# The first phase's TensorE queue: the projection of q issued ahead of two groups of transposes

## The reference

```python
h = _layernorm(x, axis=-1)
q_in = silu(causal_dwconv(h @ Wq, wq_conv))      # 4 taps
k_in = silu(causal_dwconv(h @ Wk, wk_conv))
v_in = silu(causal_dwconv(h @ Wv, wv_conv))
beta = sigmoid(h @ Wb)
q = l2norm(q); k = l2norm(k)
kb = k * beta[..., None]                         # the scaled keys
local_short = causal_dwconv(v_in, fir_short)     # 5 taps
```

## Time and profile before

| | before |
|---|---|
| median of 3 runs | 1263.83 us |
| lowest, highest | 1260.26, 1267.31 us |
| the profiled execution, own time | 1260.86 us |
| its span | 1259.1 us |
| granted TensorE clock over the span | 0.949 |
| PE, DVE, ACT, POOL busy | 1084.3, 984.7, 755.2, 645.1 us |

### The profile page before, as it was taken

The page is one execution under the profiler, slowest core; times in us unless marked ns, Lnnn a source line. Parts: engine busy times, 40 slices in busy tenths (PEclk is TensorE's granted clock), DMA queues, the critical chain, the costliest instruction groups (busy, mean ns, idle before and its releaser), DMA issues. The chain is left out here.

```text
span 1259.1 us, 28322 instructions
## 1 busy us (share of the span) xinstructions
PE 1084.3 (86%) x8715; PEld 793.7 (63%) x8799; DVE 984.7 (78%) x2955; ACT 755.2 (60%) x1456; POOL 645.1 (51%) x2360
## 2 busy tenths in 40 slices
PE   5798988596788989999999999999999977875755
PEld 4677767494456666777777677677777744542224
DVE  4899989696776887988888888898888778624975
ACT  5787878533344456666666766766666553435766
POOL 4777776415356564665656555565565644001006
PEclk9988988798899999999999999999999998897979
DMA  5666766546224254334335435434532532115006
GB/s 163 212 206 199 229 197 184 188 123 169 80 68 122 82 138 140 92 108 148 95 114 149 119 117 149 126 107 124 149 93 81 161 97 61 43 40 187 1 7 227
DMA packets 159830, 160.33 MB, mean 127 GB/s; under 512 B 65320, under 2 KB 126656, under 8 KB 159680
## 3 DMA queue, kind: packets, MB, share of 16 engines
q1 hardware_dynamic: 155552, 157.47, 41.6%
q10 hardware_dynamic: 4128, 1.05, 0.4%
HBM read 96.34 MB, written 61.87 MB: 126 GB/s over the span
## 5 line engine op out<-in xcount | busy, mean ns | idle before, releaser
L2154 DVE CUSTOM_DVE_ANT_0 x_psA<-x_psA,x_mask_q 128x256 f32<-128x256 f32 x496 | 200.6, 446 | 60.0 <-PE x_psA L1438 59.1
L1706 ACT ACTIVATE x_PT<-x_psB 128x512 f32<-128x512 f32 x240 | 143.6, 598 | 143.1 <-PE x_psB L1465 141.8
L314 DVE SCALAR_TENSOR_TENSOR a_conv<-a_ps_proj,taps,a_conv 128x253 f32<-128x253 f32 (+2 forms) x288 | 115.0, 470 | 16.7 <-ACT a_conv L381 16.7
L537 PE MATMUL a_ps_proj<-a_hT,wqkv 128*128 128x256 f32 x384 | 108.4, 432 | 9.5 <-DVE a_conv L314 6.6
L1438 PE MATMUL x_psA<-x_Ks,x_Qs 96*128 96x256 bf16 x496 | 97.6, 278 | 15.5 <-DVE x_maxima L2154 13.3
L1465 PE MATMUL x_psB<-x_Qs,x_Ks 98*128 98x256 bf16 x480 | 93.0, 274 | 10.5 <-issue 5.9
L537 PEld LDWEIGHTS a_ps_proj<-a_hT,wqkv 128*128 128x128 f32 x384 | 80.0, 219 | 29.7 <-issue 14.6
L2154 DVE DVE_READ_ACCUMULATOR2_ANT x_maxima<- 128x1 f32 x512 | 72.0, 141 | 0.0
L1479 PE MATMUL x_psO<-x_PT,x_V 128*32 128x256 f32 x1024 | 71.1, 397 | 0.7 <-ACT x_PT L1706 0.7
L2377 POOL TENSOR_TENSOR f_y<-f_y,f_x 128x512 f32<-128x512 f32 x16 | 22.9, 1454 | 87.8 <-DVE f_y L2365 80.2
L1465 PEld LDWEIGHTS x_psB<-x_Qs,x_Ks 98*128 98x128 bf16 x480 | 47.6, 99 | 32.0 <-issue 1.4
(11 more groups left out here) (385 smaller groups left out, 3256.7 us busy)
## 6 DMA issues: line engine op xcount, KB each, us to landing
scratch_keypack<-a_keypack SPq DMA_DIRECT2D x16, 768.0 KB, 3.8
c_keypack<-scratch_keypack SPq DMA_DIRECT2D x16, 768.0 KB, 4.6
x_Ks<-scratch_k_parts SPq DMA_DIRECT2D x192, 64.0 KB, 2.4
matrix<-scratch_taps_copies SPq DMA_DIRECT2D x32, 256.0 KB, 4.0
scratch_k_parts<-x_parts_k SPq DMA_DIRECT2D x32, 192.0 KB, 2.3
scratch_q_parts<-x_parts_q SPq DMA_DIRECT2D x32, 192.0 KB, 2.5
x_Qs<-scratch_q_parts SPq DMA_DIRECT2D x32, 192.0 KB, 2.9
a_x_in<-in_x SPq DMA_DIRECT2D x16, 256.0 KB, 3.7
```

The costliest lines, as they stand in the source:

```text
L314: nc.vector.scalar_tensor_tensor(acc, ps_proj[PROJ_BANK[p]][:, c, 0:L - j], taps[:, p, c, TAPS - 1 - j:TAPS - j], acc, ALU.mult, ALU.add). ...
L537: last = nc.tensor.matmul(ps_proj[PROJ_BANK[p]][:, o], wqkv[:, p, c, o * P:(o + 1) * P], hT[par][:, c], start=c == 0, stop=c == FC - 1)
L1706: nc.scalar.activation(PT[:, k % (2 * GROUP)], bank_B(b, k)[0], ACT.Exp, scale=XD ** -0.5).then_inc(pexp_ready, 1)
L2154: last = nc.vector.tensor_tensor_reduce(bank_A(b, k)[0][:, s], bank_A(b, k)[0][:, s], mask_q[:, t], 1.0, LOWEST, ALU.add, ALU.max, maxima[ ...
```

## The change

The entry of `proj_q` leaves the top of `A_ORDER`, where it stood as `(3, "proj_q")` between `kpk` and `tap_q`, and comes back as `(2, "proj_q")` between `short_t` and `stok`. Stage 2 instead of 3 and a place late in the list instead of early in the next turn mean the same batch in the same round: it is issued once per batch as before, only ahead of what used to stand between, on PE the transposes `ksT` and `tok1`. Nothing is added or removed. The rest of the difference only breaks the list's lines anew.

```diff
 A_ORDER = [
-           (5, "kpk"), (3, "proj_q"), (3, "tap_q"), (3, "conv_k"), (4, "tail"),
+           (5, "kpk"), (3, "tap_q"), (3, "conv_k"), (4, "tail"),
...
-           (4, "short_t"), (4, "stok"), (1, "xn"), (2, "gbias"), (4, "ks"), (4, "ksT"), (3, "tok1"), (3, "sq1"),
+           (4, "short_t"), (2, "proj_q"), (4, "stok"), (1, "xn"), (2, "gbias"), (4, "ks"), (4, "ksT"), (3, "tok1"), (3, "sq1"),
```

More of the change, by code:

```diff
@@ L70, in rsqrt @@
         nc.gpsimd.tensor_tensor(y, y, t, ALU.mult).then_inc(step, 1)
-A_ORDER = [(0, "ld_x"), (1, "copy"), (4, "silu_v"), (1, "rstd"), (5, "kpk"), (3, "proj_q"), (3, "tap_q"), (3, "conv_k"), (4, "tail"),
+A_ORDER = [(0, "ld_x"), (1, "copy"), (4, "silu_v"), (1, "rstd"), (5, "kpk"), (3, "tap_q"), (3, "conv_k"), (4, "tail"),
            (4, "norms"), (4, "norm"), (2, "turn_h"), (2, "hTc"), (4, "ktok"), (5, "st_p"), (4, "st_k"), (3, "taps0"),
[L77 to L80, removed]
+           (3, "conv_q"), (5, "diag"), (4, "stap"), (5, "dk"), (3, "tanh"), (3, "silu_q"), (2, "proj_k"), (4, "short1"),
+           (3, "silu_k"), (3, "proj_v"), (3, "tap_v"), (4, "tok2"), (4, "vtok"), (2, "tap_k"), (2, "gate"), (0, "stat"),
+           (4, "short2"), (3, "st_hT"), (3, "gsc"), (4, "st_v"), (4, "win"), (3, "taps1"), (3, "tok0"), (3, "sq0"),
+           (4, "short_t"), (2, "proj_q"), (4, "stok"), (1, "xn"), (2, "gbias"), (4, "ks"), (4, "ksT"), (3, "tok1"), (3, "sq1"),
            (4, "st_s"), (3, "conv_v")]
```

## The result

| | before | changed |
|---|---|---|
| median of the runs | 1265.45 us (4 runs) | 1306.39 us (4 runs) |
| lowest, highest | 1260.26, 1267.31 | 1296.52, 1310.29 |
| profiled execution, span | 1259.1 us | 1304.1 us |
| first matmul of `phase_b` | 248.2 us | 288.1 us |

The change makes the kernel slower: ratio 1.0319, 95% interval 1.028 to 1.0358, 41 us by the medians. I had forecast slower, at 1283 us, and the range ended at 1297. The direction was right; the forecast size, 21 us, was half of what came.

What follows compares the result with a forecast made beforehand. No engine is full; in the first phase they wait for one another in a ring. To 1260.9 us it added 10 (longer ring) and 11 (PE's lower clock), giving 1282; forecast 1283, range 1271 to 1297.

Steps and rivals of the forecast that it cites:

- the ring: First phase, `conv_q` to next `conv_q` through `conv_v`, `proj_q`, `ksT`, `tok1`, `sq1`, `tap_q`: 14.20 us at full clock, +10 us.
- the list of steps: The steps from one `conv_q` start to the next at full clock, from 6.42 us up to `conv_v` on, summing to 14.20 us.
- slow turns: First-phase turns with PE at its lower clock in `ksT`, `tok1`, `proj_q`: 1.68 us more each, 11 of 14 before.
- `conv_q` to the start of `conv_v`, DVE's own work without a wait: 6.42 us: First step of a first-phase turn, on DVE, taken from the trace before the change: 6.42 of 14.20 us.
- POOL sets the pace: Rival: POOL's 14.86 us from `ks` to `ks`, with a stall under DVE's `short1`, sets each turn; 1283 us, chance 0.06.
- the clock, +11: PE's lower clock in the first phase, up to 1.68 us a turn, taken in a bit under half of 14 turns.
- Every turn slow: Rival: PE's lower clock costs 1.68 us in each of 14 first-phase turns; +33.5 us, 1294; chance 0.17 (nearly all slow).
- Faster: Rival: DVE's 13.8 us wait for `tap_q` goes because the product comes first; at best 1247 us, chance 0.04.
- No turn slow: Rival: PE keeps its full clock in all or most first-phase turns; +10 to +14 us, 1271 to 1275; chance 0.17 (few slow).

Runs made afterwards that it cites:

- the square: Changed kernel with `gsc` unmoved or moved, PE idle or kept busy by unread matmuls: `phase_b` starts at 288.1, 267.8 (idle), 268.6, 258.4 us (busy).

## Why the prediction was wrong

**Right: the ring, its members and its length.** Of the list of steps only the first failed. `conv_v` to `conv_q` was 7.78 us in the sum (14.20 - 6.42) and 7.80 in the trace; the whole ring 14.20 against 14.27 in the kernel with `gsc` moved and PE kept busy; its cost over the 15 gaps +10 against +11.0 (20.64 to 232.77 us there, 212.1 against 211.2). This cost is net of the 10.6 us that the slow turns of the kernel before had taken, as in the prediction's own sum, which set full-clock turns against the 201.1 us as they were. That `tap_q` is queued behind `sq1` is shown by the ACT rows, and that the ring runs through `tok1` by the kernel with `tok1` first, which gives all of the loss back, and by 12.83 against 14.27 us a turn at full clock.

**Wrong: "`conv_q` to the start of `conv_v`, DVE's own work without a wait: 6.42 us".** It was 7.27 us in eleven turns. I took DVE's part of a turn as fixed, although the change shifts POOL's work against it: `gsc` now meets `ks` and ends only with it, 0.86 us a turn, 9.4 us by count, 10.2 by the square. I had contention only as the rival "POOL sets the pace", a DVE instruction holding a POOL one, and priced it as hidden. It came the other way round, on the engine that has no slack. `ks` began at 174.06 and ended at 175.44, `gsc` ended at 175.46. The page "SBUF — State Buffer" of the Trainium skill, section "Who interferes with whom", says that the pair of SBUF ports that VectorE and GpSimd share is an exclusive lock, that `tensor_scalar` can take it in its faster modes, and that issue order decides who blocks. The trace agrees: `ks` was first, and `gsc` ended 0.02 us behind it.

**Mis-sized: the clock, +11.** The parts above 7.80 us from `conv_v` to `conv_q` sum to 19.4 us over twelve turns. With the contention the clock cost 19.5 us. Without it, it cost 9.4 by the profiled executions, near the 11, and 2 by the medians. What failed is the share of slow turns: I took a bit under half of 14, and twelve of fifteen were slow; with `gsc` moved, five. Why the contention makes more turns slow is not shown. It lengthens the turn (15.08 against 14.26 us at full clock) and PE's wait (2.78 against 1.85 us), but by the turns named above neither of the two alone decides. "Every turn slow", to which I gave 0.17, was the better guess here, and even its +33.5 lacked the contention.

Without the contention the forecast would have stood: the kernel with `gsc` moved has `phase_b` 19.6 us later than before and a median 16 us above, and I had said 21. That is partly luck, since nothing in the rows of before fixed how many turns would be slow. The later phases took 5 us more in the profiled execution; no cause was shown.

**The other rivals.** That the clock's part was paid before as well is true of about half of it (10.6 of 19.5 us). Faster: refuted by the order on ACT, as argued; `sq1` came too late in each turn. No turn slow: refuted. POOL's pace: refuted for the changed kernel, where POOL waits 47.8 us, though POOL does set the turns of the kernel before once the clock is full.

## What to carry to other kernels

Issuing a result earlier is worth nothing if its reader is queued behind the readers of what it passes: read the consumer's queue before moving the producer's. When a move shifts engines against one another, look for every small instruction of the pair VectorE and GpSimd that will now meet a long one of the other, in both directions, on the engine without slack; and look again after the remedy, since `gsc`, moved away from `ks`, met `tail` in two later kernels. What TensorE's clock costs is not a constant per turn: small moves elsewhere changed the number of slow turns from twelve of fifteen to five, and to none in the steady part. So price it as a range, and test it with unread matmuls.

## What the runs showed of the hardware that was not expected

- A 128x16 float32 scaling on VectorE took 1.01 us instead of 0.17 beside a GpSimd multiplication of 128x512, which itself took 1.38 instead of 1.04 where it began while VectorE's `short2` ran: both were held, one after the other. Beside another GpSimd instruction, `tail` of 128x504, the same scaling took 1.00 us.
- Unread float32 matmuls in TensorE's idle time kept its granted clock at 1.00 over the steady part: the start of `phase_b` came 19.5 us earlier in the changed kernel with six matmuls a turn, and 10.6 in the kernel before with two, where the whole became 6.4 us (0.5%) faster.
- Slow and full-clock turns stand side by side in one execution with the same wait ahead of the same product (1.85 us with `gsc` moved); what decides between them is open.
